# Retention layer with an NVFP4 linear: v projected with tokens on the partitions from the second group of tokens on, and a new order of VectorE's work

## The chip, the cores and the metric

The kernel runs on one core of one Trainium2 chip. The metric is the device time of one execution, in microseconds (us); less is better. Five engines work side by side, each through its own queue: TensorE (PE in the profile; its weight loads are PEld), VectorE (DVE), ScalarE (ACT), GpSimdE (POOL), and SyncE (SP), which here issues every DMA. They wait for each other through semaphores alone.

## The reference

Over 4 x 1024 tokens of 1024 features, float32 throughout:

```
xn = layernorm(x)                                     # per token
q = (xn @ Wq + bq) * 64**-0.5;  k = xn @ Wk + bk;  v = xn @ Wv + bv      # 16 heads of 64
D[i, j] = exp(decay_h * (i - j)) for i >= j, else 0
ret = (q @ k.T) * D;  ret = ret / clip(|sum_j ret|, 1)
attn = ret @ v
g = groupnorm of attn over each head, * gn_w + gn_b
y = (silu(xn @ Wg + bg) * g) @ Wo + bo
f = nvfp4(xn) @ nvfp4(weight).T * output_scale + bias # blocks of 16, e2m1 values, e4m3 block scales
out = x + y + f
```

## The kernel before

The 4096 tokens are cut into 8 groups of 512, the 16 heads into 8 pairs of 128 features. One **body** of the loops (`body` in each engine's program) does, for one group, two pairs, `u` = 0 and 1; four bodies make a group. It also does a share of the output of the group before, and prepares 128 tokens of the group after: layernorm, the two halves of float16 parts, and the quantization to NVFP4. Bodies come in phases: FIRST (group one, 4 bodies, unrolled, in which the weights are split into float16 parts as well), SECOND and THIRD (groups two and three, 8 bodies, in which VectorE also quantizes the linear's weight matrix, one tile a body; together `QUANTIZE`), MIDDLE (groups four to eight, 20 bodies), and TAIL.

All of k, v, q and g are projected **feature-major**: `project(u, n)` (line 1288) holds a 128 x 128 piece of the weights in the array and streams 512 tokens through it, 24 matmuls (8 pieces of the contraction, three products of float16 parts), into bank `mm0` (k and q) or `mm1` (v and g). ScalarE takes the bank out with scale and bias (lines 662 and 664). For k and v the attention wants tokens on the partitions: TensorE turns them back with four float32 transposes each (`transpose_kv`, line 1298), into banks `tp0` and `tp1`, and ScalarE copies them into `kn` (line 679) and `v1` (line 687). `scores`, `state_increments`, `attend_within` and `attend_earlier` (lines 1311, 1326, 1338, 1351) are the retention. `finish_half` (line 1223) is a half of the output projection; in MIDDLE `finish_linear` (line 1232) is the linear.

VectorE does in a body: `layernorm`, `quantize_scales`, `quantize_half` twice (lines 835 to 842, seven instructions each), `mask_scores(0)` (line 1025), in QUANTIZE `f_scales`, `states(0)` (lines 1037 to 1043), in QUANTIZE `f_half(0)`, `group_norm(0)` (from line 1055; its end lets ScalarE normalize, line 695), `mask_scores(1)`, in QUANTIZE `f_half(1)`, `states(1)`, then the output additions `emit_half` (line 1163) and `emit_linear` (line 1172) with `group_norm(1)` between them. `f_half` is `quantize_half` on the weight tile. The last `emit_half` of a QUANTIZE body frees bank `mm1`, which the v projection of the next body needs. GpSimdE makes the low float16 parts (lines 539 and 564), decays q (line 546), adds biases (line 571) and multiplies by the gate (lines 556 to 559). SyncE loads each weight slice into its slot of `wring` when the projection that used the slot is done (`load_slice`, line 383).

The order on each engine is the order in which its program is written; nothing reorders it. A wait is a count in a semaphore, worked out from the table `PER` and from the use numbers in `bank_uses` and `mm_use`.

## Time and profile before

| | us |
|---|---|
| median of 3 runs (lowest, highest) | 2137.29 (2134.43, 2142.41) |
| the profiled execution's own time | 2142.48 |
| its span, first to last instruction | 2140.7 |
| busy: TensorE, VectorE, ScalarE, GpSimdE | 2080.3, 1541.7, 685.9, 640.0 |
| mean granted TensorE clock | 0.991 of 2.4 GHz |

TensorE is busy for 97% of the span. The clock row of the page has 8 or 9 tenths throughout, DMA engines are 40% busy. A busy matmul overlaps the next one in the records, so that the price of a matmul is read from the distance between two starts, not from its duration. In the rows below, a timeline row gives start and duration in us, engine, line, operation, output and inputs, and in brackets the idle time before it and what ended it. A window row gives its two ends and its length, then for TensorE, its weight loads, VectorE, ScalarE and GpSimdE the busy us with the count of instructions, then the granted clock as a share of 2.4 GHz, the DMA share and GB/s. A wait row gives the engine and line that waited, what it waited for, and us in total, times and the longest.

In the timeline of MIDDLE, bodies follow each other every 64.1 us, in QUANTIZE every 61.1 us.

### The profile page before, as it was taken

To read this page: it belongs to the slowest core of one execution; us is meant where nothing else is said; L and a number is where in the kernel's file an instruction comes from. 1 tells how busy PE (TensorE), PEld (TensorE's weight loads), DVE (VectorE), ACT (ScalarE), POOL (GpSimd) and SP (SyncE) were. 2 spreads that over 40 slices of the span, in tenths; PEclk is the share of its full clock that TensorE was granted. 3 is DMA by queue.
4 is the path that set the end of the run, shared out by engine and by line. 5 is a ranking of instruction groups with operands and counts; after the bars stand their busy time and mean duration, and the time that the engine had idled before them with its cause. 6 is when DMAs were issued, how large, how long until landed. Compare 5 with 4: busy or idle time off the path is not lost.

```text
span 2140.7 us, 51098 instructions
## 1 busy us (share of the span) xinstructions
PE 2080.3 (97%) x18098; PEld 1053.5 (49%) x18098; DVE 1541.7 (72%) x4375; ACT 685.9 (32%) x1318; POOL 640.0 (30%) x456
## 2 busy tenths in 40 slices
PE   5988899999999999999999999999999999999999
PEld 3444444455455454555555555454555454555444
DVE  7899898988889877566767556767656767656732
ACT  5756623332223233322323322323322322322300
POOL 1323232332233333223332223233223233223220
PEclk8999999999999999999999999999999999999999
DMA  8878634334343443323333323333323333223343
GB/s 317 282 253 265 218 98 138 108 109 136 100 127 108 137 128 94 102 83 109 124 103 93 103 84 109 122 103 94 103 85 107 122 103 95 103 86 106 122 153 117
DMA packets 181686, 275.61 MB, mean 129 GB/s; under 512 B 117344, under 2 KB 117472, under 8 KB 181344
## 3 DMA queue, kind: packets, MB, share of 16 engines
q1 hardware_dynamic: 181600, 274.48, 39.8%
q8 instruction: 52, 0.85, 0.2%
q14 instruction: 34, 0.28, 0.0%
HBM read 204.18 MB, written 40.89 MB: 114 GB/s over the span
## 4 chain that ended last, share of the span: by engine, by line
PE 86%; DVE 11%; DMA 2%; issue 1%; ACT 0%; SPq 0%; DVEq 0%; ACTq 0%
PE mm L1288 54%; PE mm L1223 10%; PE tp L1223 6%; PE mm L1232 4%; PE tp L1298 3%; PE four L1338 3%; PE four L1351 2%; PE tp L1326 1%; PE four L1311 1%; PE four L1232 1%; PE tp L1251 1%; DVE wo L929 1%; DMA res<-in_w_f 1%; DMA parts<-wo 1%; DVE state L1041 1%
## 5 line engine op out<-in xcount | busy, mean ns | idle before, releaser
L1288 PE MATMUL mm<-xnT,wring 128*128 128x512 f16 x6144 | 1365.8, 381 | 13.8 <-DVE wring L929 6.8
L1288 PEld LDWEIGHTS mm<-xnT,wring 128*128 128x128 f16 x6144 | 598.2, 98 | 710.3 <-issue 25.2
L695 ACT ACTIVATE work<-four,gs 128x64 f32<-128x64 f32 x512 | 158.1, 414 | 554.2 <-DVE gs L1068 554.2
L556 POOL TENSOR_TENSOR yT<-gn,gate 128x512 f32 (+1 forms) x64 | 84.2, 1315 | 800.6 <-ACT gn L706 800.6
L1223 PE MATMUL mm<-wo,yT 128*128 128x512 f16 x960 | 214.1, 380 | 0.1
L1055 DVE BATCH_NORM_STATS2 gst<-four 128x6 f32<-128x64 f32 x512 | 73.5, 216 | 195.0 <-PE four L1351 194.8
L539 POOL TENSOR_TENSOR qparts<-qT,qparts 128x512 f16<-128x512 f32 x64 | 77.0, 1203 | 363.2 <-ACT qT L664 363.1
L539 POOL TENSOR_TENSOR kparts<-kT,kparts 128x512 f16<-128x512 f32 x64 | 84.2, 1316 | 225.1 <-ACT kT L664 225.1
L1223 PEld LDWEIGHTS mm<-wo,yT 128*128 (+1 forms) x960 | 91.0, 98 | 108.3 <-issue 0.2
L1223 PE MATMUL tp<-wo,yT 128*128 128x512 f16 x576 | 128.2, 379 | 0.0
L662 ACT ACTIVATE qparts<-mm,consts,down 128x512 f16<-128x512 f32 x64 | 49.7, 776 | 213.2 <-PE mm L1288 213.2
L664 ACT ACTIVATE vT<-mm,consts,down 128x512 f32<-128x512 f32 x64 | 49.9, 780 | 208.4 <-PE mm L1288 208.4
L662 ACT ACTIVATE kparts<-mm,consts,down 128x512 f16<-128x512 f32 x64 | 50.6, 791 | 138.8 <-PE four L1311 138.8
L1039 DVE COPY state<-carry 128x65 f32 x32 | 10.5, 330 | 115.8 <-PE four L1326 115.5
L840 DVE TENSOR_TENSOR xa<-xa,xm 128x512 f32<-128x512 f32 x80 | 88.1, 1101 | 2.8
L1223 PEld LDWEIGHTS tp<-wo,yT 128*128 (+1 forms) x576 | 56.3, 98 | 68.0
L557 POOL TENSOR_TENSOR gate<-gn,gate 128x512 f32<-128x512 f32 x64 | 85.2, 1331 | 0.0
L546 POOL TENSOR_TENSOR qT<-qT,qfac 128x512 f32<-128x512 f32 x64 | 81.7, 1276 | 11.6 <-POOL qparts L539 11.0
L1232 PE MATMUL mm<-wf,xqT 128*128 128x512 bf16 x352 | 83.6, 381 | 1.2 <-DVE res L1172 1.2
L664 ACT ACTIVATE gate<-mm,consts,down 128x512 f32<-128x512 f32 x64 | 51.0, 797 | 94.0 <-PE mm L1288 93.9
L1338 PE MATMUL four<-v,probs 64*64 64x65 f32 x2048 | 76.8, 224 | 4.4 <-ACT work L695 4.1
L559 POOL TENSOR_TENSOR yT<-gate,yT 128x512 f32 (+1 forms) x64 | 74.9, 1171 | 11.4 <-POOL gate L557 10.8
(198 smaller groups left out, 2648.8 us busy)
## 6 DMA issues: line engine op xcount, KB each, us to landing
wring<-parts SPq DMA_DIRECT2D x252, 512.0 KB, 3.9
xt<-in_x SPq DMA_DIRECT2D x34, 512.0 KB, 3.6
out<-res SPq DMA_DIRECT2D x32, 512.0 KB, 3.0
parts<-wo SPq DMA_DIRECT2D x28, 512.0 KB, 5.6
res<-in_x SPq DMA_DIRECT2D x28, 512.0 KB, 3.5
ftile<-in_w_f SPq DMA_DIRECT2D x12, 512.0 KB, 4.4
parts<-wring SPq DMA_DIRECT2D x8, 512.0 KB, 6.8
probs<-in_x SPq DMA_DIRECT2D x5, 512.0 KB, 4.6
```

The lines of the kernel that those rows point to most:

```text
L539: nc.gpsimd.tensor_tensor(parts[:, 1], full, parts[:, 0], ALU.subtract)\
L546: nc.gpsimd.tensor_tensor(qT[:, u].rearrange("p (c t) -> p c t", c=CH), qT[:, u].rearrange("p (c t) -> p c t", c=CH), factor, ALU.mult).th ...
L556: nc.gpsimd.tensor_tensor(hi, gn[:], gate[:, u], ALU.mult)
L557: nc.gpsimd.tensor_tensor(gate[:, u], gn[:], gate[:, u], ALU.mult).then_inc(s["gated"], 1)
L662: nc.scalar.activation((kparts, None, qparts)[n][:, 0], mm[0][:], ACT.Identity, bias=bias[:, n, pair(u)], scale=down[:, n, pair(u)])
L664: nc.scalar.activation(dst, mm[n % 2][:], ACT.Silu if n == 3 else ACT.Identity, bias=bias[:, n, pair(u)], scale=down[:, n, pair(u)])\
L695: last = nc.scalar.activation(work[:, c * P + h * HD:c * P + (h + 1) * HD], ao[h][:, c * VW:c * VW + HD], ACT.Identity, bias=gs[:, 1, g:g ...
L840: then(V.tensor_tensor(xa[:], xa[:], xm[:], ALU.add))
L1223: last = MM(out[:], y[:, yj, k, ds(q * P, P)], wo[:, wj, k, h * GROUP:(h + 1) * GROUP], start=(n == 0), stop=(n == 3 * KT - 1))
L1232: last = MM(out, xs[:, k, :], wf[:, k, h * GROUP:(h + 1) * GROUP], start=(k == 0), stop=(k == KT - 1))
L1288: last = MM(mm[n % 2][:], wring[:, n, wj, k, :], xnT[:, parity, xj, k, :], start=(j == 0), stop=(j == 3 * KT - 1))
L1338: last = MM(ao[h][tokens(k), columns(k)], probs[tokens(k), h, k // 2, 0:SUB], v1[tokens(k), k // 2, h, :], start=(k < 2), stop=False, skip ...
```

## The change

From group two on, v is projected **token-major**: `project_v(j)` holds 128 tokens of `xnT` in the array and streams the weights of both pairs, 2 x 128 columns, so that one matmul has 256 columns, and there are 48 of them in a call, 96 in a body, in place of 48 of 512 columns. The result lies in `mm1` with tokens on the partitions. ScalarE takes it out straight into `v1` (four instructions of 256 elements in a body in place of two of 512 with bias and two copies of 512), and the bias, which now lies along the free axis, is added by GpSimdE (`bias_v`, twice a body, 512 elements). The eight v transposes of a body and `copy_v` are gone.

Since both pairs' v weights are used together, slots 1 and 3 of `wring` hold them at the start of a body; the gates' weights are loaded into the same slots when `project_v(1)` is done (`load_gates`), and the next body's v weights after each gate projection. TensorE's order is now k0, v, g transpose, q0, k0 transpose, v, k1, scores, g0, and so on. On ScalarE the gate's evacuation moves behind k1's. `state_increments(0)` waits for both bias additions. During group one, two more DMAs of 512 KB are issued (a copy of one v slice, and the bias rows); group one itself is projected as before.

On VectorE, in MIDDLE, `mask_scores(0)` moves ahead of the second half of x's quantization. In QUANTIZE it stays behind both halves; there `f_half(0)` moves from before `group_norm(0)` to behind `mask_scores(1)`, and `f_half(1)` from there to behind `emit_half(0)`, just before `group_norm(1)`.

```diff
@@ counts of semaphore steps per body, [start, group one, two, three, others, tail]
-    "t0_full": (0, 5, 5, 5, 5, 1), "t0_free": (1, 5, 5, 5, 5, 1),
-    "t1_full": (0, 3, 3, 3, 4, 1), "t1_free": (1, 3, 3, 3, 4, 1),
+    "t0_full": (0, 5, 4, 4, 4, 1), "t0_free": (1, 5, 4, 4, 4, 1),
+    "t1_full": (0, 3, 2, 2, 3, 1), "t1_free": (1, 3, 2, 2, 3, 1),
...
+    "v_ready": (0, 0, 2, 2, 2, 0),
@@ def bank_uses(phase):
-    t0 = ("k0", "u0", "v1", "u1", "g1")
-    t1 = ("v0", "k1", "g0")
+    if phase == FIRST:
+        t0, t1 = ("k0", "u0", "v1", "u1", "g1"), ("v0", "k1", "g0")
+    else:
+        t0, t1 = ("k0", "u0", "u1", "g1"), ("k1", "g0")
...
+def g_use(phase, u):
+    return mm_use(u, 3) if phase == FIRST else 3 + u
@@ buffers
-        vT = sb("vT", [P, GROUP])
+        v_bias = sb("v_bias", [P, E])
-        v1 = sb("v1", [P, CH, 2, VW])
+        v1 = sb("v1", [P, CH, 4, VW])
+        vT = xqf[:].bitcast(F32)
@@ SyncE
+                def load_gates():
+                    w("mm1_full", 2)
+                    for u in range(2):
+                        load_ring(2 * u + 1, 3, q * 2 + u)
+                def load_v(u):
+                    w("mm1_full", g_use(phase, u))
+                    load_ring(2 * u + 1, 1, q * 2 + 2 + u)
...
+                    if i == 1:
+                        sp.wait_ge(stored[5], 16)
+                        sp.dma_start(a["parts"][1, PAIRS + 1], a["parts"][1, 1]).then_inc(wrap_stored, 16)
+                        sp.dma_start(v_bias[:], a["bv"]).then_inc(v_bias_in, 16)
...
-                for n in range(4):
-                    load_slice(0, n)
+                load_slice(0, 0)
+                load_slice(0, 2)
+                load_gates()
                 move_x_parts()
                 w("xq_ready", 1)
                 load_x(1)
-                for n in range(4):
-                    load_slice(1, n)
+                load_slice(1, 0)
+                load_v(0)
+                load_slice(1, 2)
+                load_v(1)
@@ GpSimdE
+                def bias_v(j):
+                    w("mm1_free", j + 1)
+                    out = v1[:, 2 * j:2 * j + 2, :, 0:HD]
+                    rows = v_bias[:, ds(q * (2 * P), 2 * P)].rearrange("p (h d) -> p h d", d=HD)
+                    nc.gpsimd.tensor_tensor(out, out, rows.unsqueeze(1).broadcast_to([P, 2, 4, HD]), ALU.add)\
+                      .then_inc(s["v_ready"], 1)
...
                 split(1, kT[:], kparts)
+                if phase != FIRST:
+                    bias_v(0)
                 split(2, qT[:, 0], qparts)
                 decay_q(0)
                 x_lo()
+                if phase != FIRST:
+                    bias_v(1)
                 split(3, kT[:], kparts)
@@ ScalarE
+                def evacuate_v(j):
+                    w("within", 0)
+                    w("mm1_full", j + 1)
+                    for u in range(2):
+                        from_u = mm[1][:].rearrange("p (c a h d) -> p c a h d", c=2, a=2, d=HD)[:, :, u]
+                        last = nc.scalar.activation(v1[:, 2 * j:2 * j + 2, 2 * u:2 * u + 2, 0:HD], from_u,
+                                                    ACT.Copy, scale=down[:, 1, pair(u)])
+                    last.then_inc(s["mm1_free"], 1)
...
                 evacuate(0, 0)
-                evacuate(0, 1)
+                evacuate_v(0)
                 affine(1, 1)
                 x_hi()
                 evacuate(0, 2)
-                copy_v(0)
                 decay_k(0)
+                evacuate_v(1)
+                evacuate(1, 0)
                 evacuate(0, 3)
-                evacuate(1, 0)
-                evacuate(1, 1)
                 decay_k(1)
                 evacuate(1, 2)
-                copy_v(1)
@@ VectorE
                 quantize_half(xt, 0)
-                quantize_half(xt, 1)
+                if phase in QUANTIZE:
+                    quantize_half(xt, 1)
                 mask_scores(0)
                 if phase in QUANTIZE:
                     f_scales()
+                else:
+                    quantize_half(xt, 1)
                 states(0)
-                if phase in QUANTIZE:
-                    f_half(0)
                 group_norm(0)
                 mask_scores(1)
                 if phase in QUANTIZE:
-                    f_half(1)
+                    f_half(0)
                 states(1)
                 emit_half(w, 0, "mm0", 5)
                 if phase == MIDDLE:
                     emit_linear(w, 0, "mm1", 5, "mm0", 5)
+                else:
+                    f_half(1)
                 group_norm(1)
@@ TensorE
+                def project_v(j):
+                    if j == 0:
+                        w("w_v", 0)
+                        w("w_g", 0)
+                    w("mm1_free", j)
+                    out = mm[1][:].rearrange("p (c a x) -> p c a x", c=2, a=2)
+                    for c in range(2):
+                        tokens = slice((2 * j + c) * P, (2 * j + c + 1) * P)
+                        n = 0
+                        for k in range(KT):
+                            for wj, xj in ((0, 0), (1, 0), (0, 1)):
+                                last = MM(out[:, c], xnT[:, parity, xj, k, tokens], wring[:, 1::2, wj, k, :],
+                                          start=(n == 0), stop=(n == 3 * KT - 1))
+                                n += 1
+                    last.then_inc(s["mm1_full"], 1)
...
                 def state_increments(u):
...
+                    if phase != FIRST:
+                        w("v_ready", 2)
```

TensorE's rows at the head of a THIRD body (`kT` and `vT` are k and v with features on the partitions, `mm` the projection banks, `tp` the transpose banks), before:

```order
L296 ISA x2
L1288 MATMUL mm<-xnT,wring 128x512 x48
L296 ISA
L296 REGISTER_ALU
L1251 MATMUL tp<-consts,work 128x128 x4
L296 REGISTER_ALU
L1288 MATMUL mm<-xnT,wring 128x512 x24
L296 ISA
L1298 MATMUL tp<-consts,vT 128x128 x4
L296 REGISTER_ALU
L1298 MATMUL tp<-consts,kT 128x128 x4
L1288 MATMUL mm<-xnT,wring 128x512 x24
```

and after:

```order
L308 ISA x2
L1356 MATMUL mm<-xnT,wring 128x512 x24
L1373 MATMUL mm<-wring,xnT 128x256 x48
L308 ISA x2
L1316 MATMUL tp<-consts,work 128x128 x4
L308 REGISTER_ALU
L1356 MATMUL mm<-xnT,wring 128x512 x24
L308 REGISTER_ALU
L1383 MATMUL tp<-consts,kT 128x128 x4
L1373 MATMUL mm<-wring,xnT 128x256 x48
L308 REGISTER_ALU x2
L1356 MATMUL mm<-xnT,wring 128x512 x24
```

The second projection is 48 matmuls of 256 columns, the v transposes are gone, and the place of g0 is taken by the second half of v.

VectorE's rows at the end of a THIRD body, from the last step of `states(1)` to the first instruction of `group_norm(1)` (`carry` is the running state, `res` the output tile, `ftile` the weight tile, `four` holds the attention), before:

```order
L1043 ISA
L1043 SCALAR_TENSOR_TENSOR carry<-state,lam,four 128x65
L296 REGISTER_ALU
L1163 SCALAR_TENSOR_TENSOR res<-mm,cols,res 128x512
L296 REGISTER_ALU
L1055 BN_STATS gst<-four 128x6 x8
```

and after:

```order
L1228 SCALAR_TENSOR_TENSOR res<-mm,cols,res 128x512
L897 TENSOR_TENSOR xa<-ftile,qs 128x512
L846 REGISTER_ALU
L898 TENSOR_SCALAR xa<-xa 128x512
L846 REGISTER_ALU
L900 TENSOR_SCALAR xm<-xa 128x512
L846 REGISTER_ALU
L901 TENSOR_SCALAR xm<-xm 128x512
L846 REGISTER_ALU
L902 TENSOR_TENSOR xa<-xa,xm 128x512
L846 REGISTER_ALU
L903 TENSOR_TENSOR xa<-xa,xm 128x512
```

Line 904, which writes the tile's second half, and then line 1117, the first of `group_norm(1)`, follow. Seven instructions of VectorE now stand between the first output addition and the second group norm.

GpSimdE's rows at the head of a THIRD body after the change (`v` is `v1`); before, the two splits of line 577 stood next to each other:

```order
L577 TENSOR_TENSOR kparts<-kT,kparts 128x512
L618 ISA
L618 TENSOR_TENSOR v<-v,v_bias 128x8x64
L308 REGISTER_ALU
L577 TENSOR_TENSOR qparts<-qT,qparts 128x512
```

The bias addition stands between the split of k and that of q, on which `scores(0)` waits; the second one follows the low part of x.

## Rows read from the trace of the kernel before

**Rows 1.** The page: busy time, share of the span, instructions

```profile
PE 2080.3 (97%) x18098; PEld 1053.5 (49%) x18098; DVE 1541.7 (72%) x4375; ACT 685.9 (32%) x1318; POOL 640.0 (30%) x456
```

**Rows 2.** Groups of weight loads: count, busy us, mean ns, idle before

```profile
L1288 PEld LDWEIGHTS mm<-xnT,wring 128*128 128x128 f16 x6144 | 598.2, 98 | 710.3 <-issue 25.2 <-DVE wo L929 2.9 <-DVE res L1163 0.5
...
L1298 PEld LDWEIGHTS tp<-consts,vT 128*128 128x128 f32 x256 | 29.5, 141 | 8.3
```

**Rows 3.** Windows, a MIDDLE body and six QUANTIZE bodies: busy us, clock, DMA

```profile
826.91:891.02 64.11, 64.11 (x569) 32.46 (x568) 42.06 (x125) 18.55 (x37) 19.65 (x14) 1.00 0.32 102
395.73:762.58 366.85, 365.24 (x3280) 184.61 (x3281) 321.28 (x869) 111.29 (x222) 120.07 (x84) 1.00 0.39 120
```

**Rows 4.** Timeline of TensorE, one MIDDLE body: start, duration

```profile
1542.97 5.34 PE L1288 MATMUL mm<-xnT,wring 128*128 128x512 f16 x24
1548.15 0.60 PE L1298 MATMUL tp<-consts,vT 128*128 128x128 f32 x4
1548.58 0.60 PE L1298 MATMUL tp<-consts,kT 128*128 128x128 f32 x4
...
1573.24 0.66 PE L1298 MATMUL tp<-consts,vT 128*128 128x128 f32 x4
1573.74 5.34 PE L1288 MATMUL mm<-xnT,wring 128*128 128x512 f16 x24
```

**Rows 5.** Timeline of VectorE, one THIRD body

```profile
517.87 1.15 DVE L1055 BATCH_NORM_STATS2 gst<-four 128x6 f32<-128x64 f32 x8 [1.47 <-PE four L1351]
...
522.55 0.74 DVE L1163 SCALAR_TENSOR_TENSOR res<-mm,cols,res 128x512 f32<-128x512 f32 x1
...
547.26 0.75 DVE L1025 TENSOR_TENSOR probs<-four,dmask 128x256 f32<-128x256 f32 x2
...
552.12 0.23 DVE L1037 COPY state<-tp 128x65 f32<-128x65 f32 x1 [0.35 <-PE four L1326]
...
559.45 1.15 DVE L1055 BATCH_NORM_STATS2 gst<-four 128x6 f32<-128x64 f32 x8 [0.48 <-PE four L1351]
...
568.16 0.76 DVE L1025 TENSOR_TENSOR probs<-four,dmask 128x256 f32<-128x256 f32 x2
568.83 0.68 DVE L835 TENSOR_TENSOR xa<-ftile,qs 128x512 f32<-128x512 f32 x1
...
573.00 0.22 DVE L1037 COPY state<-tp 128x65 f32<-128x65 f32 x1
...
575.60 0.74 DVE L1163 SCALAR_TENSOR_TENSOR res<-mm,cols,res 128x512 f32<-128x512 f32 x1
579.08 1.15 DVE L1055 BATCH_NORM_STATS2 gst<-four 128x6 f32<-128x64 f32 x8 [2.74 <-PE four L1351]
```

**Rows 6.** Timeline of ScalarE and TensorE, the same body

```profile
568.16 2.48 ACT L695 ACTIVATE work<-four,gs 128x64 f32<-128x64 f32 x8 [7.26 <-DVE gs L1068]
...
570.93 0.60 PE L1251 MATMUL tp<-consts,work 128*128 128x128 f32 x4
```

**Rows 7.** Timeline of VectorE and GpSimdE, one MIDDLE body

```profile
1551.65 1.69 DVE L840 TENSOR_TENSOR xa<-xa,xm 128x512 f32<-128x512 f32 x1
...
1558.74 0.69 DVE L840 TENSOR_TENSOR xa<-xa,xm 128x512 f32<-128x512 f32 x1
...
1551.52 1.27 POOL L546 TENSOR_TENSOR qT<-qT,qfac 128x512 f32<-128x512 f32 x1 [0.20 <-POOL qparts L539]
```

**Rows 8.** Waits of TensorE, 178 to 192 us and 299 to 306 us

```profile
PE tp L1326 <- DVE probs L1025: 2.9, 1, 2.9
...
PE tp L1326 <- DVE probs L1025: 2.6, 1, 2.6
```

**Rows 9.** Windows around these two waits, columns as in rows 3

```profile
180.00:190.00 10.00, 7.11 (x92) 4.17 (x91) 9.42 (x28) 1.71 (x4) 1.70 (x1) 1.00 0.73 131
300.00:310.00 10.00, 7.42 (x86) 4.44 (x85) 8.95 (x24) 1.62 (x3) 0.00 (x0) 0.83 0.67 236
```

**Rows 10.** DMA issues: KB each, median us to landing

```profile
wring<-parts SPq DMA_DIRECT2D x252, 512.0 KB, 3.9
```

More of the change, by code:

```diff
@@ L399, in store_late, with load_ring @@
                     sp.dma_start(a["out"][ds(j * GROUP + i * P, P), :], late_bufs[j][:]).then_inc(late_out[j], 16)
+                def load_ring(n, matrix, pair):
+                    src = a["parts"][matrix, ds(pair, 1)].rearrange("a p n -> p (a n)")
+                    sp.dma_start(wring[:, n].rearrange("p a b c -> p (a b c)"), src)\
+                      .then_inc(s["w_" + MATS[n]], 16)
+                def load_gates():
[5 more added lines that the diff above has]
+                    load_ring(2 * u + 1, 1, q * 2 + 2 + u)
                 if phase == TAIL:
@@ L651, in evacuate @@
                 def evacuate(u, n):
-                    use = mm_use(u, n)
+                    use = g_use(phase, u) if n == 3 else mm_use(u, n)
                     w(f"mm{n % 2}_full", use)
-                    dst = (kT[:], vT[:], qT[:, u], gate[:, u])[n]
+                    dst = (kT[:], vT, qT[:, u], gate[:, u])[n]
                     if n == 3:
@@ L702, in affine @@
                     bk, use = bank_uses(phase)[f"g{u}"]
-                    w(f"t{bk}_full", use - 5 * back)
+                    w(f"t{bk}_full", 0 if back else use)
                     w("gated", u - 2 * back)
@@ L1248, in transpose_g @@
                     w("normed", u + 1 - 2 * back)
-                    w(f"t{bk}_free", use - 1 - 5 * back)
+                    w(f"t{bk}_free", -1 if back else use - 1)
                     for c in range(CH):
@@ L1277, in project @@
                 def project(u, n):
-                    use = mm_use(u, n)
+                    use = g_use(phase, u) if n == 3 else mm_use(u, n)
+                    slot = n
+                    if n == 3 and phase != FIRST:
+                        slot = 2 * u + 1
                     if (phase, i, u) == (FIRST, 0, 0):
@@ L1287, in project @@
                         for wj, xj in ((0, 0), (0, 1), (1, 0)):
-                            last = MM(mm[n % 2][:], wring[:, n, wj, k, :], xnT[:, parity, xj, k, :],
+                            last = MM(mm[n % 2][:], wring[:, slot, wj, k, :], xnT[:, parity, xj, k, :],
                                       start=(j == 0), stop=(j == 3 * KT - 1))
@@ L1313, in scores, with v_head @@
                     last.then_inc(s["scores_full"], 1)
+                def v_head(u, h):
+                    return h if phase == FIRST else 2 * u + h
                 def state_increments(u):
                     bk, use = uses[f"u{u}"]
-                    for which in "kv":
+                    for which in ("kv" if phase == FIRST else "k"):
                         b, n = uses[f"{which}{u}"]
                         w(f"t{b}_free", n)
+                    if phase != FIRST:
+                        w("v_ready", 2)
                     w(f"t{bk}_free", use - 1)
@@ L1360, in body @@
                     sum_slices(0, 4, 4)
-                project(0, 1)
+                if phase == FIRST:
+                    project(0, 1)
+                else:
+                    project_v(0)
                 if phase != FIRST or i:
@@ L1364, in body @@
                 project(0, 2)
-                transpose_kv(0, "v", vT, 1)
+                if phase == FIRST:
+                    transpose_kv(0, "v", vT, 1)
                 transpose_kv(0, "k", kT, 0)
-                project(0, 3)
+                if phase == FIRST:
+                    project(0, 3)
+                else:
+                    project_v(1)
                 project(1, 0)
@@ L1375, in body @@
                     sum_slices(i + 1, 0, SLICES)
-                project(1, 1)
+                if phase == FIRST:
+                    project(1, 1)
+                else:
+                    project(0, 3)
                 if phase == FIRST and i == 0:
```

46 lines of the change are left out of this document (29 added, 17 removed).

## The prediction, made before the changed kernel ran

> **What bounds the kernel now.** I read the page's first part, then windows, then the timeline of one body on each engine. TensorE is busy for 97% of the span [rows 1]. A MIDDLE body of 64.11 us has TensorE busy for all of it and VectorE for 42.06; the six QUANTIZE bodies of the second row take 61.14 us each (366.85 / 6), TensorE idles 0.27 us in each, and VectorE is busy for 321.28 of 366.85, 88% [rows 3]. So in MIDDLE each microsecond taken from TensorE counts in full, as long as nobody else becomes late; in QUANTIZE VectorE is close behind, and the same saving has to be asked of it too. The reader is to see in the timeline that VectorE, in spite of its 88%, waits before the second group norm of a body: 2.74 us [rows 5]. That idle time is the reserve which the change spends.
>
> **TensorE's own work.** Distances between starts give the prices. Four v transposes take 1548.58 - 1548.15 = 0.43 us in front of the k transposes and 1573.74 - 1573.24 = 0.50 behind the retention step; both go: -0.93 us a body [rows 4]. The k transposes stay.
>
> The v projections were 48 matmuls of 512 columns, 24 of them in 1548.15 - 1542.97 = 5.18 us, 0.2158 each, 10.36 in all [rows 4]. Now they are 96 of 256 columns, each with its own weight load. No such matmul is in the trace. Below, the price is half of 0.2158, 0.1079 (the same number of columns): no change. The nearest row for a short matmul that brings a full 128 x 128 load each time is the float32 transpose, 4 in 0.43 us, 0.1088 each [rows 4], though its load takes 141 ns where a float16 one takes 98 [rows 2]; the loads thus lie behind each other's matmuls. I take 0.1088: 96 x 0.1088 = 10.44, +0.08 us a body. Above, if a load could not start before the last one has ended and took the 141 ns: 96 x 0.141 = 13.5, +3.2 us a body. With 98 ns loads it would still hide, by 11 ns.
>
> The Trainium skill (TensorE: Matmul & The Clock Gate, section Back-to-back issue gap) has another rule for streams of load and matmul: some 81 ns a matmul at 128 columns and 131 at 512. An estimate between these, 98 ns at 256, would make v 9.4 us and the change 1.0 us a body better. The trace has 0.2158 at 512 columns, not 0.131 [rows 4]; the measurement decides, and I give this no chance.
>
> Net for TensorE: -0.93 + 0.08 = -0.85 us a body. In MIDDLE that is 20 x 0.85 = -17.0.
>
> **What covers the rest in MIDDLE.** Times from the start of a body, in the new order. The gates' weights are asked for when the second v call is done and are needed after k1's 24 matmuls and the scores, over 5.18 us later [rows 4]; a slice lands after 3.9 [rows 10]. Covered, with 1.3 or more to spare, less if the second load of the pair slows the first. ScalarE has four pieces of 256 elements in place of four of 512: cheaper. The bias additions have the size of the decay of q, 1.27 us on GpSimdE [rows 7], and stand beside the splits of k and q, for which the scores wait. Between the freeing of q0's bank and the scores lie now the second v call and k1, over 10 us; three works of 1.3 fit into them. But while GpSimdE works, VectorE is slower: the same addition took 1.69 us beside it and 0.69 alone [rows 7]. So each bias addition takes up to 1.0 from VectorE, 2.0 a body, not below 0. In MIDDLE the first mask no longer waits for the second half of the quantization, so it gains more than this; the half that comes after it has until the retention of pair 0. Cost nothing; without the move it would still be covered, VectorE having 22 idle us a body [rows 3]. SyncE passes the gates' loads before the x parts, as it passed g0's before.
>
> The Trainium skill (GPSIMD Engine Reference, Key points) says that the two engines share SBUF interfaces and contend where a VectorE instruction has two SBUF inputs or runs in a two-port mode. By that rule the two bias additions speak against this change; the pair of rows agrees, with 1.69 against 0.69 us.
>
> **QUANTIZE.** Here `f_half(1)` now stands between the first output addition and `group_norm(1)`, and the last output addition behind that frees the bank which the next body's v projection needs. Follow VectorE from the start of `group_norm(0)`, which waits for TensorE (attend_earlier), at 559.45 [rows 5]. To the end of the first output addition: 575.60 + 0.74 - 559.45 = 16.89 us, without an idle moment; the same instructions are there after the change, with `f_half(0)` where `f_half(1)` was. Then `f_half(1)`, 573.00 - 568.83 = 4.17. Then group norm and output addition, 522.55 + 0.74 - 517.87 = 5.42. Sum 26.48; I add 0.2 for the gate's products on GpSimdE, which run up to this point (0 to 1.0, one addition slowed). From the freed bank to the next `group_norm(0)` TensorE is the slower: 559.45 - 523.29 = 36.16 before [rows 5], less 0.43 for the one v transpose within, plus 0.08: 35.81. The new body is 26.68 + 35.81 = 62.5 us against 61.14: +1.4 us a body (at least +1.2, with the 1.0 +2.2). Without VectorE's limit it would be 61.14 - 0.85 - 0.2 = 60.1, so that TensorE now waits 2.4 us a body. The reserve of 2.74 us was smaller than the 4.17 put into it. Of this, 0.2 falls on the group norm's transpose: ScalarE's normalization ends at 568.16 + 2.48 = 570.64, TensorE came at 570.93 [rows 6] and now comes 0.50 earlier. The rest is at the first v projection.
>
> Eight bodies: 8 x 1.4 = +11.2.
>
> In the first of these bodies VectorE arrives late from group one and TensorE waits for the mask, 2.6 us [rows 8]. The bias additions fall into the quantization before it: up to +2.0, I take +1.3, once. In the other bodies the mask is done at 547.26 + 0.75 = 548.01, and the increments, which wait for it, end just before 552.12 [rows 5]: over 3 us of slack, against 2.0.
>
> **The clock.** The granted clock stood at 2.4 GHz throughout in the window with the wait of 2.9 us, and at 0.83 in the one with the wait of 2.6 [rows 8, 9]: such a wait sometimes brings 1.2 GHz. A mean of 0.83 over 10 us is 3.4 us at half speed, at most 1.7 us lost. For eight new waits of 2.2 I take one such loss, rounded to +2 with its aftermath.
>
> **Group one.** Two more DMAs of 512 KB, where nobody waits for their data before the next group: 0, at most +1.
>
> **Sum.** -17.0 + 11.2 + 1.3 + 2 = -2.5 us on the profiled execution's own 2142.48: 2140.0. The median stood at 2137.29, 0.9976 of it: 2135.
>
> **Rivals.**
>
> *VectorE's chain doesn't bind.* If the group norm could end without the moved half on the path, all 28 bodies would gain 0.85 and eight their 0.2 wait: -25.4, 2112. For it speaks only that VectorE waits for TensorE in front of both group norms [rows 5]; against it, the sum of durations above, in an order that nothing changes.
>
> *The chain is longer and the clock falls with it.* The mechanism of the forecast with its upper price: +1.0 in place of 0.2 for GpSimdE makes the wait at the v projection 3.0 us, beyond the 2.6 after which the clock fell. Then each of the eight bodies loses 0.8 + 1.7 more: 2135 + 20 - 2 = 2153. It decides from the point at which most waits are 2.6 us or longer. For it: waits of that length were followed by a low clock in one of two windows [rows 9]. Against it: the gate's products overlapped only the end of the half before, and cost it nothing visible.
>
> *Short matmuls don't hide their loads.* At 141 ns: 28 x 3.1 = +87, 2222; it reaches break-even, from the forecast, at 0.1097 us a matmul (0.09 us more a body), which is only 1% above my price, so that a small miss here moves the time by a few us within the range: 115 ns would be 28 x 0.6 = +17, 2152. Against it: the 0.1088 of a matmul with a longer load.
>
> **How the numbers follow.** Forecast 0.66, own range 2125 to 2147; chain not binding 0.14; long chain with the clock 0.13; loads not hidden 0.07. Range 2110 to 2154: it takes in the first two rivals and leaves out the far part of the third, and tails. This kernel's measurement can tell about 0.5%, 10.7 us, from no change. Faster by more than that (below 2126.6): 0.14 + 0.07 of the forecast = 0.21. Slower (above 2148.0): 0.12 + 0.06 + 0.02 = 0.20. Same: 0.59.
>
> **What would show it.** In the profile after: 2688 matmuls of 256 columns (28 x 96) at 0.109 us from start to start, none at 0.14; v transposes left only in group one (32 instead of 256). MIDDLE bodies of 63.3 us with TensorE never waiting. QUANTIZE bodies of 62.5, with a wait of about 2.2 us at the first matmul of the v projection, released by VectorE's output addition, and VectorE without idle time between the two group norms. If instead these bodies take 60.1, the chain was read wrongly; if MIDDLE bodies show waits for `wring` or for `v_ready`, the covers were. The time is wrong above all if the matmul price is, since it is paid 2688 times.

## The result, and the profile after

| | before | after |
|---|---|---|
| median (lowest, highest), 8 runs each, us | 2139.11 (2134.43, 2143.22) | 2145.52 (2144.49, 2147.81) |
| span of the profiled execution | 2140.7 | 2144.3 |
| TensorE, VectorE, GpSimdE busy | 2080.3, 1541.7, 640.0 | 2056.5, 1636.5, 742.4 |

The changed kernel takes 1.0031 of the time before, 95% interval 1.0018 to 1.0045. The forecast was a hair faster (2135.0, 0.9989 of the 2137.29 it was made against); the kernel became a little slower. The time lies in the range given, which is wide enough for that; the direction was wrong. The two kinds of bodies, MIDDLE and QUANTIZE, pull in opposite directions, and each by more than their sum.

The page of the changed kernel, busy time, share of the span and instructions, against [rows 1]:

```profile
PE 2056.5 (96%) x19174; PEld 1162.6 (54%) x19218; DVE 1636.5 (76%) x4375; ACT 663.1 (31%) x1318; POOL 742.4 (35%) x512
```

TensorE has 24 us less to do and is nonetheless done later. VectorE has the same 4375 instructions and is busy 95 us longer. Without GpSimdE's bias additions (e5, below) it is busy 1599.5 us, so that they make 37 of the 95; the rest is not taken apart here.

The length of a body is read as the distance between the gate transposes of its pair 1 and those of the body after it. In us:

| body | before | after | each | in all |
|---|---|---|---|---|
| SECOND, the first | 66.2 | 73.05 | +6.8 | +6.8 |
| SECOND, three more | 61.17 | 65.1 | +3.9 | +11.8 |
| THIRD, four | 61.1 | 62.6 | +1.4 | +5.8 |
| MIDDLE, twenty | 64.11 | 63.29 | -0.82 | -16.5 |

That makes +7.9; the medians differ by 6.4. (The two profiled executions differ by 3.6 only: group one, which computes the same in both, ended 3.4 us earlier in the changed kernel's, and the end after the last body is 0.9 us shorter. Over the traces of all runs group one ended between 272.4 and 278.9 us.)

Windows of the changed kernel, columns as in [rows 3]: two SECOND bodies one by one, four THIRD bodies together, a MIDDLE body.

```profile
413.50:478.60 65.10, 61.94 (x594) 35.38 (x592) 56.50 (x146) 17.73 (x37) 24.18 (x16) 0.97 0.36 112
478.60:543.60 65.00, 61.85 (x594) 35.24 (x593) 56.51 (x147) 17.74 (x37) 24.17 (x16) 0.97 0.35 111
543.60:794.00 250.40, 241.18 (x2339) 138.00 (x2338) 221.70 (x575) 70.92 (x148) 93.58 (x64) 1.00 0.37 115
826.91:890.20 63.29, 62.97 (x608) 36.22 (x609) 46.66 (x127) 17.73 (x37) 23.06 (x16) 1.00 0.34 105
```

The reader is to see the clock column: 0.97 in the SECOND bodies, 1.00 in the others. TensorE's waits, 280 to 800 us, with the total, the times and the longest; before, no wait at a projection in this stretch was longer than 0.3, and the mask's was 2.6 [rows 8]:

```profile
PE mm L1373 <- DVE res L1228: 18.3, 8, 2.8
PE tp L1416 <- DVE probs L1087: 4.2, 1, 4.2
PE mm L1356 <- issue: 1.9, 8, 0.3
PE tp L1316 <- ACT work L759: 0.9, 4, 0.2
```

TensorE's timeline, the second v projection of a body in which nothing is waited for, then the first one of a SECOND and of a THIRD body:

```profile
419.76 5.40 PE L1373 MATMUL mm<-wring,xnT 128*128 128x256 f16 x48
425.00 5.34 PE L1356 MATMUL mm<-xnT,wring 128*128 128x512 f16 x24
...
471.94 7.07 PE L1373 MATMUL mm<-wring,xnT 128*128 128x256 f16 x48 [2.64 <-DVE res L1228]
478.85 0.60 PE L1316 MATMUL tp<-consts,work 128*128 128x128 f32 x4
...
663.83 5.40 PE L1373 MATMUL mm<-wring,xnT 128*128 128x256 f16 x48 [1.88 <-DVE res L1228]
669.06 0.60 PE L1316 MATMUL tp<-consts,work 128*128 128x128 f32 x4
```

48 matmuls take 5.24 us undisturbed (0.109 each), 5.23 behind a wait of 1.88, and 6.91 behind one of 2.64. The same work costs 1.68 us more, and windows show why: the granted clock is 0.83 over the ten microseconds around that place (part of them at 1.2 GHz), and 1.00 behind another THIRD body's wait of 1.88, which ended at 601.22.

```profile
467.00:477.00 10.00, 7.36 (x43) 4.80 (x42) 8.55 (x44) 3.81 (x10) 0.00 (x0) 0.83 0.50 132
...
600.00:610.00 10.00, 8.78 (x67) 6.62 (x68) 8.84 (x29) 6.27 (x14) 1.49 (x2) 1.00 0.59 210
```

Why the wait is longer in SECOND stands in VectorE's timeline, from the first instruction of `group_norm(0)` to the last output addition. A SECOND body:

```profile
444.19 1.15 DVE L1117 BATCH_NORM_STATS2 gst<-four 128x6 f32<-128x64 f32 x8 [3.83 <-PE four L1441]
...
457.10 0.69 DVE L904 TENSOR_TENSOR xqf<-xa,qs 128x512 bf16<-128x512 f32 x1
458.03 0.94 DVE L1101 COPY state<-carry 128x65 f32 x1 [0.24 <-DVE xqf L904]
...
461.55 0.75 DVE L1228 SCALAR_TENSOR_TENSOR res<-mm,cols,res 128x512 f32<-128x512 f32 x1
462.22 0.68 DVE L897 TENSOR_TENSOR xa<-ftile,qs 128x512 f32<-128x512 f32 x1
...
466.38 1.14 DVE L1117 BATCH_NORM_STATS2 gst<-four 128x6 f32<-128x64 f32 x8
471.05 0.74 DVE L1228 SCALAR_TENSOR_TENSOR res<-mm,cols,res 128x512 f32<-128x512 f32 x1
```

And a THIRD body:

```profile
636.91 1.15 DVE L1117 BATCH_NORM_STATS2 gst<-four 128x6 f32<-128x64 f32 x8 [2.01 <-PE four L1441]
...
650.66 0.23 DVE L1099 COPY state<-tp 128x65 f32<-128x65 f32 x1
...
658.26 1.14 DVE L1117 BATCH_NORM_STATS2 gst<-four 128x6 f32<-128x64 f32 x8
...
662.94 0.74 DVE L1228 SCALAR_TENSOR_TENSOR res<-mm,cols,res 128x512 f32<-128x512 f32 x1
...
699.51 1.15 DVE L1117 BATCH_NORM_STATS2 gst<-four 128x6 f32<-128x64 f32 x8 [2.03 <-PE four L1441]
```

In both the second group norm starts without idle time, where it waited 2.74 us before [rows 5]. The chain is 662.94 + 0.74 - 636.91 = 26.77 us in THIRD and 471.79 - 444.19 = 27.60 in SECOND, where `states` begins with a copy of the running state (line 1101, 0.94 us beside the gate product of GpSimdE, for the 0.23 of line 1099) and has one step more. GpSimdE's timeline, the SECOND body:

```profile
457.28 1.63 POOL L594 TENSOR_TENSOR yT<-gn,gate 128x512 f32 x1 [7.15 <-ACT gn L770]
```

The way back, from the freed bank (663.68, the end of the last output addition) to the next `group_norm(0)`, is 699.51 - 663.68 = 35.83; chain and way back make the 62.60 of the body.

### The profile page after: what moved, and what is told of

It is laid out like the page before. It is cut to its first block, busy times and chain, and to the rows that moved or that the text cites. A ratio compares the mean times of both kernels' runs of the same rounds, so it can differ in the third digit from the quotient of the medians.

```text
span 2144.3 us, 53432 instructions
## 1 busy us (share of the span) xinstructions
PE 2056.5 (96%) x19174; PEld 1162.6 (54%) x19218; DVE 1636.5 (76%) x4375; ACT 663.1 (31%) x1318; POOL 742.4 (35%) x512
## 4 chain that ended last, share of the span: by engine, by line
PE 77%; DVE 17%; issue 3%; DMA 2%; ACT 0%; SPq 0%; DVEq 0%
PE mm L1356 38%; PE mm L1373 14%; PE mm L1288 6%; PE tp L1288 6%; PE mm L1297 3%; PE four L1428 2%; PE tp L1383 1%; PE four L1441 1%; PE tp L1416 1%; DVE state L1103 1%; PE four L1297 1%; PE four L1396 1%; DVE gst L1117 1%; DVE wo L991 1%; DVE xa L897 1%
## 5 line engine op out<-in xcount | busy, mean ns | idle before, releaser
L1356 PE MATMUL mm<-xnT,wring 128*128 128x512 f16 x4800 | 1072.0, 380 | 13.7 <-DVE wring L991 7.6
L1356 PEld LDWEIGHTS mm<-xnT,wring 128*128 128x128 f16 x4800 | 464.8, 98 | 549.5 <-issue 17.2
L1373 PE MATMUL mm<-wring,xnT 128*128 128x256 f16 x2688 | 309.1, 276 | 18.3 <-DVE res L1228 18.3
L1373 PEld LDWEIGHTS mm<-wring,xnT 128*128 128x128 f16 x2688 | 265.7, 99 | 59.5 <-issue 19.7
L744 ACT ACTIVATE v<-mm,down 128x256 f32<-128x256 f32 x112 | 47.1, 474 | 192.7 <-PE mm L1373 144.2
L901 DVE TENSOR_SCALAR xm<-xm 128x512 f32<-128x512 f32 x80 | 97.9, 1223 | 2.8
L903 DVE TENSOR_TENSOR xa<-xa,xm 128x512 f32<-128x512 f32 x80 | 94.2, 1178 | 2.7
L902 DVE TENSOR_TENSOR xa<-xa,xm 128x512 f32<-128x512 f32 x80 | 80.9, 1011 | 2.8
```

The lines of the kernel that those rows point to most:

```text
L901: then(V.tensor_scalar(xm[:], xm[:], 1.0, 1.5 * 2.0 ** 22, ALU.max, ALU.mult))
L903: then(V.tensor_tensor(xa[:], xa[:], xm[:], ALU.subtract))
L1356: last = MM(mm[n % 2][:], wring[:, slot, wj, k, :], xnT[:, parity, xj, k, :], start=(j == 0), stop=(j == 3 * KT - 1))
L1373: last = MM(out[:, c], xnT[:, parity, xj, k, tokens], wring[:, 1::2, wj, k, :], start=(n == 0), stop=(n == 3 * KT - 1))
```

## The experiments

Ratios are against the kernel before, run beside each version on the same chip: its medians there were 2138.3 to 2140.1 us.

### e3: the halves alone

The kernel before, with nothing but the move of the weight tile's halves.

```diff
                 states(0)
-                if phase in QUANTIZE:
-                    f_half(0)
                 group_norm(0)
                 mask_scores(1)
                 if phase in QUANTIZE:
-                    f_half(1)
+                    f_half(0)
                 states(1)
...
+                else:
+                    f_half(1)
                 group_norm(1)
```

> The kernel before with only the two moves of f_half in SECOND and THIRD; v is projected as before, no bias additions on GpSimdE. Theory: the chain of 26.5 us (27.7 in SECOND, with its longer states) plus 36.2 on TensorE: THIRD 62.8 us in place of 61.1, SECOND 64 and with a fall of the clock 65.6; 4 x 1.7 + 4 x 4.4 = 24 us slower than before, 2163, ratio 1.011; MIDDLE unchanged at 64.1. Rival (GpSimdE's bias additions and the v projection's own waits made the bodies longer): unchanged, 2139, ratio 1.000.

Measured: 2161.08 (2160.15 to 2163.2), ratio 1.0105 [1.0089, 1.012]. Bodies 70.5, 63.8 and twice 65.4 in SECOND, 63.0 in THIRD, 64.11 in MIDDLE. Its waits, same stretch:

```profile
PE mm L1288 <- DVE res L1163: 18.3, 8, 2.8
PE tp L1326 <- DVE probs L1025: 2.6, 1, 2.6
```

The theory (2163) was right. The move makes nearly the whole loss of QUANTIZE (22.7 us over the eight bodies, 24.4 in the changed kernel), with the same 18.3 us of waiting at the same place, without any v projection of the new kind. TensorE at two of the SECOND waits:

```profile
405.60 5.34 PE L1288 MATMUL mm<-xnT,wring 128*128 128x512 f16 x24 [2.62 <-DVE res L1163]
...
469.38 7.03 PE L1288 MATMUL mm<-xnT,wring 128*128 128x512 f16 x24 [2.63 <-DVE res L1163]
```

Behind the first the clock stayed at 2.4 GHz, and that body took 63.8 us; behind the second it fell, and that body took 65.4. The waits are equal to 0.01 us: whether the clock falls behind one of 2.6 us is not settled by its length, and the fall costs 1.6 to 1.7 us.

### e6: VectorE in its old order

The changed kernel, with all of VectorE's work in the order of before.

```diff
-                if phase in QUANTIZE:
-                    quantize_half(xt, 1)
+                quantize_half(xt, 1)
                 mask_scores(0)
                 if phase in QUANTIZE:
                     f_scales()
-                else:
-                    quantize_half(xt, 1)
                 states(0)
+                if phase in QUANTIZE:
+                    f_half(0)
                 group_norm(0)
                 mask_scores(1)
                 if phase in QUANTIZE:
-                    f_half(0)
+                    f_half(1)
...
-                else:
-                    f_half(1)
                 group_norm(1)
```

> VectorE wholly in its old order: both halves of f_half back, and in MIDDLE the first mask behind both halves of x's quantization again; the v projection as changed. Theory (in MIDDLE the mask's move is worth nothing, as VectorE has the time): MIDDLE bodies 63.3 as in the kernel with the halves back, 2131. Rival (with the bias additions the mask is late without its move): MIDDLE bodies 64 or more, 20 x 0.7 = 14 us more, 2145.

Measured: 2155.64 (2154.97 to 2160.19), ratio 1.0085 [1.0067, 1.0103]. Eleven of the twenty MIDDLE bodies take 65.2 to 66.9 us, the others 63.3. Its waits, 800 to 2100 us:

```profile
PE tp L1413 <- DVE probs L1087: 21.1, 11, 2.2
```

And VectorE in one of the other nine bodies, where the mask ends (1574.92) only 0.8 us before TensorE's increments start (1575.75); in a MIDDLE body of the kernel before it was 3.7 us (1561.55 and 1565.27):

```profile
1572.73 1.53 DVE L904 TENSOR_TENSOR xq<-xa,qs 128x512 bf16<-128x512 f32 x1
1574.18 0.74 DVE L1087 TENSOR_TENSOR probs<-four,dmask 128x256 f32<-128x256 f32 x2
1576.51 0.23 DVE L1099 COPY state<-tp 128x65 f32<-128x65 f32 x1 [1.59 <-PE four L1413]
```

I had held the move of the mask to be worth nothing, and that fell: the new v projection needs it. Against e1, which differs in that alone, it is worth 24.9 us. The rival had 2145, the right kind of result and too small a size.

### e1: the halves back in their old places

```diff
                 states(0)
+                if phase in QUANTIZE:
+                    f_half(0)
                 group_norm(0)
                 mask_scores(1)
                 if phase in QUANTIZE:
-                    f_half(0)
+                    f_half(1)
                 states(1)
...
-                else:
-                    f_half(1)
                 group_norm(1)
```

> The changed kernel with f_half(0) and f_half(1) of SECOND and THIRD back where they were before (ahead of group_norm(0), and between mask_scores(1) and states(1)); all else as changed. Theory (VectorE's chain from group_norm(0) to the last output addition sets these bodies, and the clock falls after its long waits): TensorE sets the bodies again, THIRD 60.3 us in place of 62.6, SECOND 60.5 in place of 65.1, no wait of 2 us at the v projection; 4 x 4.6 + 4 x 2.3 = 28 us below the changed kernel, about 2118, ratio to before 0.990. Rival (it is GpSimdE's bias additions, which slow VectorE, that lengthen these bodies): they stay, so the time stays within 8 us of 2145, ratio 1.000 or more.

Measured: 2130.73 (2126.63 to 2133.37), ratio 0.9964 [0.9951, 0.9978]; bodies 68.8, 62.1 in SECOND, 61.9 to 62.15 in THIRD, 63.29 in MIDDLE. The version beats both kernels, but of the 28 us below the changed kernel that the theory expected only 15 are there, and the rival (within 8 us of 2145) missed too. The bodies got shorter, so the halves' place is what made them long; but the wait did not go, it moved to the gate transposes, which wait for ScalarE's normalization behind `group_norm(0)`:

```profile
PE tp L1316 <- ACT work L759: 10.3, 8, 1.6
...
PE mm L1373 <- DVE res L1228: 0.2, 1, 0.2
```

### e2: one half back, the other left behind the output addition

```diff
                 states(0)
+                if phase in QUANTIZE:
+                    f_half(0)
                 group_norm(0)
                 mask_scores(1)
-                if phase in QUANTIZE:
-                    f_half(0)
                 states(1)
```

> The changed kernel with only f_half(0) put back ahead of group_norm(0); f_half(1) stays just before group_norm(1). Theory (the sum of the chain counts: 4.17 us less between the two group norms leaves idle time before the second again): bodies as with both halves back, THIRD 60.3, SECOND 60.5, about 2118, ratio 0.990. Rival (it is the place of f_half(1), right before the group norm that the next v projection waits for, that costs): the wait at the v projection stays, 2138 or more, ratio 1.000.

Measured: 2141.57, ratio 1.0014 [1.0004, 1.0024]; bodies 70.2, 63.55 and 63.34. The theory's 2118 is missed by 24 us, the rival was right. The kernel has both waits, 12.0 us at the projection and 10.3 at the gate transposes. VectorE in a THIRD body shows the error:

```profile
576.88 0.76 DVE L1087 TENSOR_TENSOR probs<-four,dmask 128x256 f32<-128x256 f32 x2
580.82 0.23 DVE L1099 COPY state<-tp 128x65 f32<-128x65 f32 x1 [3.19 <-PE four L1416]
...
584.12 1.53 DVE L897 TENSOR_TENSOR xa<-ftile,qs 128x512 f32<-128x512 f32 x1
...
589.13 1.14 DVE L1117 BATCH_NORM_STATS2 gst<-four 128x6 f32<-128x64 f32 x8
```

Between the mask and `states(1)` are 3.19 us in which VectorE waits for TensorE's increments. From the mask to the copy it is 3.94 us here, and 4.83 in e1, where a half stands between them (568.11 to 572.94 in its trace): there the half costs VectorE's chain 0.9 us. Behind the output addition it costs the whole 5.0 from 584.12 to 589.13. The body is 1.4 to 1.5 us longer than in e1. Where idle time lies decides, not how much of it a body has.

### e4: the clock taken out of it

The changed kernel, with eight unread matmuls of 512 columns before the first v projection of every QUANTIZE body, into a free bank: TensorE has work while it would wait.

```diff
+                        if phase in QUANTIZE:
+                            w("t1_free", 0)
+                            for k in range(8):
+                                MM(tp[1][:], xnT[:, parity, 0, k, 0:P], xnT[:, parity, 0, k, :], start=True, stop=True)
```

> The changed kernel with 8 matmuls of 512 columns more, whose result nobody reads (into the free transpose bank), ahead of the first v projection of each SECOND and THIRD body: 1.7 us of work inside a wait of 1.9 to 2.8. Theory (in SECOND the clock falls after the wait of 2.6 us or more, and the v projection then takes 6.9 us in place of 5.24): the clock stays up, SECOND bodies go from 65.1 to 63.5, THIRD stays at 62.6, about 6 us faster than the changed kernel, 2139, ratio 1.000. Rival (the v projection of SECOND is long for another reason, as the arrival of its weights): SECOND stays at 65.1, no gain, ratio 1.003.

Measured: 2139.62, ratio 1.0004 [0.9995, 1.0014]. SECOND bodies fall from 65.1 to 63.4, the first from 73.05 to 69.8, THIRD stays (62.54), as the theory had it. TensorE around the place:

```profile
463.77 1.89 PE L1369 MATMUL tp<-xnT 128*128 128x512 f16 x8
466.50 5.41 PE L1377 MATMUL mm<-wring,xnT 128*128 128x256 f16 x48 [0.84 <-DVE res L1228]
471.75 0.60 PE L1316 MATMUL tp<-consts,work 128*128 128x128 f32 x4
```

The eight (1.89 us) and what is left of the wait (0.84) are together as long as the wait was (2.64), so the projection starts no earlier; but it takes 5.25 us instead of 6.91. So 1.7 us of each steady SECOND body were the clock, and VectorE's lateness the rest. The first body gains 3.2: 1.7 at its projection, and the rest elsewhere, in part by a shorter low clock behind the mask's wait, which this edit does not touch. Work without any use makes this kernel 5.9 us faster, and as fast as the one before, not faster.

### e5 and e7: without the bias additions

The additions of v's bias on GpSimdE are left out of the changed kernel (e5) and of e1 (e7); their output lacks that bias.

```diff
-                    nc.gpsimd.tensor_tensor(out, out, rows.unsqueeze(1).broadcast_to([P, 2, 4, HD]), ALU.add)\
-                      .then_inc(s["v_ready"], 1)
+                    pool.sem_inc(s["v_ready"], 1)
```

> The changed kernel without the two bias additions of v on GpSimdE (v's bias is left out of the result; the semaphore is raised by a plain increment). Theory (VectorE is idle 2 to 4 us before group_norm(0) in SECOND and THIRD, which hides what the additions cost it, and the chain from there to the last output addition has no bias addition in it): bodies stay at 65.1, 62.6 and 63.3; only the first SECOND body, whose mask is late by 4.2 us, gains about 2; 2143. Rival (the additions slow VectorE on the path): every SECOND and THIRD body gains 1 us or more, 2136 or less.

> The kernel with both halves of f_half put back, and also without the bias additions of v on GpSimdE (v's bias is left out of the result). With the halves back, TensorE waits 1.6 us in each SECOND and THIRD body for group_norm(0)'s transpose, since f_half(0) ends after attend_earlier(0). Theory (the bias additions make VectorE 2.3 us later there, and this is what keeps these bodies at 62.0): without them 60.5 us, the wait under 0.4, 8 x 1.5 = 12 us and 2 of the first body below 2131, about 2117, ratio 0.990. Rival (the shorter way of TensorE to the transpose, 0.50 us less, and nothing of GpSimdE): a gain under 4 us, 2127 or more.

Measured, e5: 2143.42, ratio 1.0024 [1.0014, 1.0033]; bodies 70.35, 64.9, 62.62. The theory was right: the bias bears on the first body, where the mask is late (wait of 2.9 instead of 4.2), and on the steady SECOND ones by 0.2 us. e7: 2119.91, ratio 0.9913 [0.9896, 0.9929]; bodies 66.75, 60.8, MIDDLE 63.29; near the theory's 2117 and 60.5, and the rival (2127 or more) is out. A THIRD body of e1 and then one of e7:

```profile
651.58:713.44 61.86, 60.27 (x586) 34.50 (x585) 54.54 (x145) 17.70 (x37) 23.59 (x16) 1.00 0.38 117
```

```profile
647.75:708.53 60.78, 60.27 (x586) 34.47 (x585) 53.18 (x145) 17.69 (x37) 20.02 (x14) 1.00 0.40 121
```

Same instructions on TensorE and VectorE; without the two additions VectorE is busy 1.36 us less and the body is 1.1 us shorter. With the halves as in the changed kernel the additions cost next to nothing in the steady bodies, since idle time before `group_norm(0)` covers them; with the halves back they cost 10.8 us in all.

### e8: each half cut in two

The seven instructions of a half are cut after the fourth, and the pieces spread over the three places.

```diff
                 if phase in QUANTIZE:
+                    f_half(0, (0,))
                 group_norm(0)
                 mask_scores(1)
-                    f_half(0)
+                    f_half(0, (1,))
+                    f_half(1, (0,))
                 states(1)
...
-                    f_half(1)
+                    f_half(1, (1,))
                 group_norm(1)
```

> The changed kernel with each f_half of SECOND and THIRD cut in two pieces of about 2.1 us (four and three instructions): the first piece of f_half(0) ahead of group_norm(0), its second and the first of f_half(1) between mask_scores(1) and states(1), the last ahead of group_norm(1). Theory (the chain from group_norm(0) to the last output addition has to fit beside TensorE's 19.3 us to attend_earlier(1), and nothing more than 2 us fits ahead of group_norm(0)): chain 19.0 us in THIRD and 20.2 in SECOND, so THIRD bodies 60.5, SECOND 61.5, clock at full speed but for the first body; about 14 us less than with the halves merely back... 8 x 1.2 = 10 to 12 us less, 2120, ratio 0.991. Rival (each further piece meets a GpSimdE work and is slowed by 1 us, so that cutting gains nothing): bodies 62 as with the halves back, 2131, ratio 0.996.

Measured: 2131.59 (2130.53 to 2134.41), ratio 0.9969 [0.9958, 0.998]: like e1. THIRD gains (61.4), SECOND loses (62.4).

```profile
PE mm L1378 <- DVE res L1233: 9.3, 8, 1.8
...
PE tp L1321 <- ACT work L759: 1.0, 4, 0.3
```

Cutting turns one wait into the other, about 10.4 us in all in both kernels. The theory's 2120 is missed by 12 us, and the rival's time was right. Its reason is seen only in part: in a THIRD body one instruction of the four pieces, line 901, takes 1.47 us beside GpSimdE in place of 0.43.

### e9 and e10: the first mask ahead in every body

e1 and e8 with the mask between the halves of x in QUANTIZE as well, as it is in MIDDLE.

```diff
-                if phase in QUANTIZE:
-                    quantize_half(xt, 1)
                 mask_scores(0)
+                quantize_half(xt, 1)
                 if phase in QUANTIZE:
                     f_scales()
-                else:
-                    quantize_half(xt, 1)
```

> The halves of the weight tile as in e1, and the first mask ahead of the second half of x's quantization in every body, not in MIDDLE alone. Theory: in the steady QUANTIZE bodies the first mask has slack, so that its place there changes nothing (62.1 us as in e1); but in the first SECOND body TensorE waits 4.2 us for it in e1. Five instructions of the half and two of the scales leave its way, over 4 us with the slowed ones, so the wait goes, and with it the low clock behind it: that body falls from 68.8 to 63 or 64, five us less in all: 2130.7 - 5 = 2126, ratio 0.994. Rival: VectorE is late in that body by its whole work; then what was a wait for the mask is a wait for the group norm or at the v projection behind it, and the body stays at 68 to 69: 2131, 0.9964.

> The same move of the first mask in the kernel with the cut halves (e8). Theory: first SECOND body from 68.7 to about 64, the others as in e8 (62.4 and 61.4): 2131.6 - 5 = 2127, ratio 0.9945. Rival as in e9: the lateness only changes its place, 2131 to 2132, 0.997.

Measured, e9: 2159.3, ratio 1.0094 [1.0078, 1.0109]; bodies 68.8, then 65.6 to 67.2. e10: 2132.09, ratio 0.9966 [0.9954, 0.9978]; bodies 67.55, 63.0, 61.9. In the first body the rival was right, the mask's wait (4.2 to 0.4) came back as one of 3.4 us for the running state. In the steady bodies of e9 both were wrong, by 33 and 28 us in the time. Its VectorE and GpSimdE, a THIRD body:

```profile
560.27 0.75 DVE L1087 TENSOR_TENSOR probs<-four,dmask 128x256 f32<-128x256 f32 x2 [1.29 <-PE four L1393]
560.95 0.68 DVE L897 TENSOR_TENSOR xa<-xt,qs 128x512 f32<-128x512 f32 x1
...
577.23 2.80 POOL L609 TENSOR_TENSOR res<-res,out_bias 128x1024 f32<-128x1024 f32 x1
577.85 2.73 DVE L904 TENSOR_TENSOR xqf<-xa,qs 128x512 bf16<-128x512 f32 x1
580.77 1.15 DVE L1117 BATCH_NORM_STATS2 gst<-four 128x6 f32<-128x64 f32 x8 [0.19 <-DVE xqf L904]
```

VectorE now stands idle for 1.29 us until TensorE has the scores, the second half of x comes after, and all that is on the way to `group_norm(0)`. The larger part comes behind it: `f_half(0)`, started later, runs beside three of GpSimdE's works and takes 8.1 us (572.51 to 580.58), where in e1 only its last instruction is slowed and it takes 5.1. TensorE waits 3.5 to 3.7 us for the group norm in the seven steady bodies, and the granted clock fell at each of these waits. A step that waits for TensorE should not be called before the work that could be done in its wait; in MIDDLE, with 17 idle us of VectorE in a body, the same order is right.

## Why the prediction was wrong, step by step

**TensorE's own work: right.** The new matmul costs 0.109 us (taken: 0.1088), its loads hide; v transposes are left in group one alone. MIDDLE bodies take 63.29 (63.26 worked out), and TensorE waits for no other engine there. -16.5 against -17.0.

**What covers the rest in MIDDLE: right in its outcome, wrong in a reason.** Nothing waits for `wring` or `v_ready`, and the slices land after 4.1 us (3.9 before). But "without the move it would still be covered, VectorE having 22 idle us a body" is refuted by e6. The idle time of a body lay behind the mask, not before it, and 3.7 us of margin were not enough: in eleven bodies the mask came 1.8 to 2.2 us too late.

**QUANTIZE: the mechanism right, a term too small.** For a THIRD body the numbers came out: chain 26.77 (26.68), way back 35.83 (35.81), body 62.6 (62.5), wait 1.9 at the projection (2.2) and 0.2 at the gate transposes (0.2). This sum was made once and multiplied by eight. It fails in "Eight bodies: 8 x 1.4": SECOND's `states` copies the running state first, and its chain is 27.60, 0.9 longer than the 26.68. The trace of before had it to read, in a SECOND body, against 0.22 us in the THIRD body that was read:

```profile
450.67 1.26 DVE L1039 COPY state<-carry 128x65 f32 x1
```

**The clock: the largest term of the miss.** "For eight new waits of 2.2 I take one such loss." The waits were not equal. In THIRD they are 1.9 and cost only themselves; in SECOND they are 2.6 to 2.8 and in this trace each of the four brings 1.2 GHz and 1.7 us, as e4 shows by filling them. This is near the second rival, with 0.9 (from the copy, not from a slowed `f_half(0)`) in place of its 0.8 and with its 1.7 (0.9 + 1.7 = 2.6 on top of the 62.5 us: 65.1, as measured), holding in one half of the bodies; it was priced for all eight or none. For the three steady SECOND bodies that is 7.8 us. The clock does not make the wrong direction alone: without its fall behind these waits (e4) the kernel takes 1.0004 of the time before, the same, where a gain was forecast.

**The first SECOND body: +6.8, where 1.3 was taken beside the common 1.4.** The mask's wait rose by 1.6, close to what was thought; e5 gives 1.3 of it to the bias additions. The wait of 2.8 at its projection and the clock behind it add 4.5, less 0.85 of TensorE's work; the rest, about 1.5, is waiting for k and q at its head (0.9) and a longer low clock behind the mask, 0.66 here against 0.83 in the same window before [rows 9]:

```profile
300.00:310.00 10.00, 6.50 (x79) 4.80 (x80) 8.92 (x25) 1.05 (x3) 0.00 (x0) 0.66 0.48 160
```

This was read from the traces and not tested. It varies: in e4 the mask's wait is as long, 4.24 us, and the same window has 0.83.

**The sum.** MIDDLE -16.5 (-17.0), THIRD +5.8 (+5.6), SECOND +18.6 (5.6 + 1.3 + 2 = +8.9). The last difference, 9.7, makes with the two small ones +7.9 of the -2.5: some 3.6 of it is the longer chain (4 x 0.9), 4.8 the clock (4 x 1.7 where 2 was taken), the rest the first body. The parts taken alone do not add up to the whole: e3 has +22.8 us for the halves, e1 -7.5 for the v projection with the mask, 15.3 together against the 6.4 measured. The eight QUANTIZE bodies account for it: the v projection makes them 8.6 us longer with the halves in their old places (e1 against before) and 1.7 with the halves moved (the changed kernel against e3), because the bias additions cost 10.8 us in the one order and next to nothing in the steady bodies of the other (e7, e5). The prediction priced them for MIDDLE and for the first mask only.

## What to carry to other kernels

Ahead of moving a step, work out the chain for every kind of body that the loop has, not for the one at hand: a copy and one step more made four waits 0.8 us longer, and a wait of 2.6 us on TensorE can cost more than itself. Idle time has a place: a step costs little where its engine waits for another, and is paid in full one place later (0.9 against 5.0 us of VectorE's chain in e1 and e2). And a step that only moves work may be the condition of another part (the mask here): judge it with that part in place.

## What the runs showed of the hardware

In the changed kernel TensorE's granted clock stayed at 2.4 GHz behind the THIRD bodies' waits of 1.9 us and fell to 1.2 behind each of the waits of 2.6 to 2.8 us in the SECOND bodies, at a price of 1.7 us each; eight unread matmuls in the wait kept it. Over all twelve traces, from 150 to 2060 us, the clock fell in or within 5 us behind 30 of the 40 waits of 2.5 to 3.3 us, 1 of the 24 of 1.8 to 2.2 (1.95 us, in e6) and none of the 44 of 1.25 to 1.8. So longer waits bring it more often, and between 1.9 and 3.2 us the length alone does not tell. The Trainium skill (TensorE: Matmul & The Clock Gate, section What's actually happening) says that the clock follows how busy the engine has been recently; e4 agrees with that.

A float16 matmul of 256 columns with its own 128 x 128 load takes 0.109 us, about half of the 0.2158 of one of 512 columns, though its load takes 99 ns: the two overlap at this size too.

A VectorE instruction beside one of GpSimdE's can take until shortly after that has ended: line 904 takes 0.69 us alone and 1.53, 2.50 or 2.73 beside GpSimdE; the one of 2.73 in e9 ends at 580.58, GpSimdE's work beside it at 580.03. Two additions of 1.4 and 1.6 us on GpSimdE cost VectorE 1.4 us a body (e1 against e7). The copy at the head of `states` shows whose reads matter: from `carry` it took 0.20 us alone and 0.94 and 1.26 beside GpSimdE, from the bank `tp` 0.23 although GpSimdE worked beside it (650.03 to 651.66 us in the changed kernel's trace).
